# A new issue order of four engines in a fused attention-and-experts layer

## The reference, cut to what matters

```python
xn = layernorm(x)
q, k, v = split(xn @ W_qkv.T + b)            # 8 heads of 16
q, k, v = unit_length(q, k, v) * exp(i phase)
q, k = entangle(q), entangle(k)              # 3 depths, each head controlled by the one before it
for c in range(4):                           # 4 circuits
    s = |conj(q_i) . k_j|**2 * gain[c]       # 8 x 8 heads of one row
    w = sqrt(softmax(s) + 1e-12)
    out += sup[c] * clip(|sum_j w_ij v_j|) * its sign and phase
x + out @ W_out.T + b_out + experts(xn)
```

## Time and profile before

| what | value |
|---|---|
| median of 3 runs | 1520.07 us (1517.04 to 1521.86) |
| the profiled execution | 1518.64 us |
| its span, first to last instruction | 1516.9 us |
| granted TensorE clock, mean | 0.881 |
| busy, share of the span: VectorE, TensorE, ScalarE, GpSimd | 83%, 74%, 53%, 50% |
| opening, until block 0's first product | 111.1 us |
| steps between the first products of two blocks | 78 to 103 us |

### The profile page before, as it was taken

One profiled execution on the slowest core, in us unless ns is written; L12 is line 12 of the kernel. 1 busy time (PEld: TensorE's weight loads), 2 busy tenths in 40 slices (PEclk: granted clock), 3 DMA queues, 4 the chain that ended last, 5 costly groups with the idle time before them and its releaser, 6 DMA issues.

```text
span 1516.9 us, 19541 instructions
## 1 busy us (share of the span) xinstructions
PE 1118.7 (74%) x6049; PEld 867.6 (57%) x6049; DVE 1257.8 (83%) x1530; ACT 799.7 (53%) x1626; POOL 764.1 (50%) x596
## 2 busy tenths in 40 slices
PE   4476687968878797867969696784977878597734
PEld 2335475856657575655747475572755657475632
DVE  4634989898987998878988989696789998799975
ACT  3424466575646565464656656373545657365321
POOL 2073433365654455375455445647724545554683
PEclk9966798999989998888989899797989989899867
DMA  7333232342525252241423334152332516242111
GB/s 214 99 99 94 56 107 76 102 130 57 148 63 150 56 153 78 81 139 53 149 78 109 87 101 120 39 163 74 114 98 56 147 44 180 53 136 79 32 38 35
DMA packets 111559, 147.40 MB, mean 97 GB/s; under 512 B 15776, under 2 KB 85088, under 8 KB 110944
## 3 DMA queue, kind: packets, MB, share of 16 engines
q1 hardware_dynamic: 102240, 125.15, 27.6%
q0 software_dynamic: 8192, 16.79, 3.4%
q10 hardware_dynamic: 1024, 4.20, 2.1%
HBM read 113.95 MB, written 32.14 MB: 96 GB/s over the span
## 4 chain that ended last, share of the span: by engine, by line
PE 51%; POOL 13%; issue 12%; ACT 11%; DVE 10%; DMA 2%; SPq 1%; ACTq 0%; DVEq 0%; POOLq 0%
PE ps_t L739 8%; PE ps_r L788 8%; PE ps_h L660 7%; PE ps_f L668 6%; PE ps_q L739 6%; PE ps_t L746 4%; POOL prod L1276 3%; PE ps_k L726 3%; POOL rows_in L1302 3%; POOL got L1317 3%; POOL sqx L1267 2%; ACT hid L1124 2%; DVE pat L1697 1%; POOL prod L1284 1%; DVE xy L1489 1%
## 5 line engine op out<-in xcount | busy, mean ns | idle before, releaser
L1284 POOL TENSOR_TENSOR prod<-expo,vT 128x512 f32<-128x512 f32 x192 | 237.1, 1269 | 138.4 <-DVE u L1697 98.0
L788 PE MATMUL ps_r<-sqx,mats 128*128 128x512 f32 x256 | 163.8, 773 | 186.1 <-POOL sqx L1267 164.7
L1276 POOL TENSOR_TENSOR prod<-kq 128x1024 f32<-128x1024 f32 x64 | 150.0, 2366 | 291.7 <-ACT kq L1059 291.6
L1124 ACT ACTIVATE hid<-ps_h,w_tile 128x128 f32<-128x128 f32 x624 | 178.0, 370 | 145.7 <-PE ps_h L660 144.5
L660 PEld LDWEIGHTS ps_h<-turned,w_tile 128*128 128x128 f32 x1248 | 173.3, 208 | 79.1 <-issue 54.2
L1697 DVE TENSOR_REDUCE pat<-prod 128x128 f32<-128x2048 f32 x96 | 217.1, 2276 | 0.5
L660 PE MATMUL ps_h<-turned,w_tile 128*128 128x128 f32 x1248 | 182.4, 293 | 39.5 <-issue 19.9
L788 PEld LDWEIGHTS ps_r<-sqx,mats 128*128 128x128 f32 x256 | 54.2, 235 | 244.5 <-POOL sqx L1267 170.2
L1267 POOL TENSOR_TENSOR sqx<-sqx,sqy 128x512 f32<-128x512 f32 x64 | 87.3, 1384 | 204.6 <-ACT sqy L1039 143.7
L1673 DVE TENSOR_TENSOR prod<-expo,ps_v 128x2048 f32<-128x2048 f32 x80 | 180.7, 2280 | 7.8 <-PE ps_t L739 6.3
L1668 DVE TENSOR_TENSOR prod<-ps_q,kq 128x1024 f32<-128x1024 f32 x128 | 150.4, 1216 | 38.4 <-PE ps_q L844 21.4
(11 more groups left out here) (267 smaller groups left out, 2130.8 us busy)
## 6 DMA issues: line engine op xcount, KB each, us to landing
w_tile<-w_cat SPq DMA_DIRECT2D x156, 514.0 KB
x_tile<-rows_in SPq DMA_DIRECT2D x156, 64.0 KB, 2.8
rows_out<-turned SPq DMA_DIRECT2D x156, 64.0 KB
rows_in<-u SPq DMA_DIRECT2D x2, 2496.0 KB, 11.9
yacc<-in_L_attn_query_dram SPq DMA_DIRECT2D x16, 256.0 KB, 4.3
out_dram<-yacc SPq DMA_DIRECT2D x16, 256.0 KB, 3.1
x_sb<-in_L_attn_query_dram SPq DMA_DIRECT2D x11, 256.0 KB, 4.2
b_tile<-b_parts SPq DMA_DIRECT2D x156, 0.8 KB
```

Of the source, the lines that this page charges most:

```text
L788: nc.tensor.matmul(ps_r[:, bank, :], m, sqx[:, g, :], start=True, stop=True).then_inc(sig.sem, 1)
L1124: act.activation(hid[:, n % 2, c, :], ps_h[:, c, :], ACT.Gelu, bias=w_tile[:, n % WS, HID + HC * C + c:HID + HC * C + c + 1]).then_inc(hid ...
L1276: last = pool.tensor_tensor(set_of(2, part), q, other, ALU.mult)
L1284: last = pool.tensor_tensor(dst[:, at], w[:, at], v[:, at], ALU.mult)
```

## The change

Only the order of calls in the four loops differs; no call is added or dropped, and SyncE's list is the same. The lines with a minus are taken out where they stand, those with a plus put in; `if exists(...)` guards and lines that stay are mostly left out.

```diff
@@ TensorE
-k_operands(k, 1)
+q_operands(k, 1)
 sum_rows(routed)
+k_operands(k, 1)
+tiles(k, 0, 1)
+k_operands(k, 2)
 rank_rows(routed)
-q_operands(k, 1)
-tiles(k, 0, 1)
-k_operands(k, 2)
 tiles(k, 1, 2)
 q_operands(k, 2)
-tiles(k, 2, 3)
+k_operands(k, 3)
 mix_circuits(o)
-tiles(k, 3, 4)
+tiles(k, 2, 3)
 control_tiles(n)
+tiles(k, 3, 4)
+q_operands(k, 3)
 target_tiles(n)
-q_operands(k, 3)
 turn_m(o)
-k_operands(k, 3)
-tiles(k, 4, 5)
 project_out(o)
+tiles(k, 4, 5)
 grow_once(n)
 turn_x(j)
 grow_once_more(n)
 tiles(k, 5, 6)
+score(j)
 grow_twice(n)
 tiles(k, 6, 7)
 grow_twice_more(n)
 sums(k, ("weighted", 0))
 sums(k, ("weighted", 1))
 k_operands(n, 0)
-score(j)
 sums(k, ("weighted", 2))
 project(far, [0, 1])
-tiles(k, 7, 8)
-project(far, [2])
 q_operands(n, 0)
-sums(k, ("weighted", 3))
+tiles(k, 7, 8)
+project(far, [2])
 tiles(k, 8, 9)
 project(far, [3])
+sums(k, ("weighted", 3))
 tiles(k, 9, None)
@@ ScalarE
+copy_tile(k, 1)
 copy_sums(routed)
-copy_tile(k, 1)
-copy_v(k)
-tiles(k, 0, 1)
 abs_sign(o, 3)
+tiles(k, 0, 1)
+norm_sqrt(n)
+copy_v(k)
 router_softmax(routed)
-tiles(k, 1, 2)
+copy_tile(k, 2)
 ln_sd(j)
-norm_sqrt(n)
-copy_tile(k, 2)
+tiles(k, 1, 2)
+copy_tile(k, 3)
 tiles(k, 2, 3)
-tiles(k, 3, 4)
 control0(n)
-copy_tile(k, 3)
-tiles(k, 4, 5)
+tiles(k, 3, 4)
 copy_mT(o)
 control1(n)
+pass_first(n)
+tiles(k, 4, 5)
 layer_norm(j)
-pass_first(n)
 copy_out(o)
+turn(n)
+control2(n)
+score_exp(k)
+pass_last(n)
 copy_xT(j)
-turn(n)
-score_exp(k)
-control2(n)
-pass_last(n)
 tiles(k, 5, 6)
...
 tiles(k, 8, 9)
-abs_sign(k, 1)
 copy_proj(far, [3])
+abs_sign(k, 1)
 tiles(k, 9, None)
@@ GpSimd
+gather(first of the step)
 products(k, ("pattern", 2))
 scatter_part(k, 0)
-gather(first of the step)
 products(k, ("pattern", 5))
 sum_squares(n, sq1_ready, sum1_ready)
+gather(second and third of the step)
 scatter_part(k, 1)
 sum_squares(n, sq2_ready, sum2_ready)
-gather(second and third of the step)
+scatter_part(k, 2)
 products(k, ("weighted", 4))
 products(k, ("weighted", 5))
-scatter_part(k, 2)
+products(k, ("weighted", 6))
 scatter_part(k, 3)
-products(k, ("weighted", 6))
 gather(fourth of the step)
@@ VectorE
 products(k, ("pattern", 0))
+sums(k, ("pattern", 0))
 route(routed)
-layer_norm_stats(j)
 sums(o, ("weighted", 6))
-sums(k, ("pattern", 0))
+layer_norm_stats(j)
 norm_squares(n)
 products(k, ("pattern", 1))
+clip_and_mix(o)
 row_numbers(routed)
-clip_and_mix(o)
 normalise(n)
-sums(k, ("pattern", 2))
-products(k, ("pattern", 3))
 invert_sd(j)
+products(k, ("pattern", 3))
+route_gates(routed)
 measure(o)
+sums(k, ("pattern", 2))
 sums(k, ("pattern", 1))
-sums(k, ("pattern", 3))
 spread(n)
 products(k, ("pattern", 4))
+sums(k, ("pattern", 3))
 sums(k, ("pattern", 4))
...
 turned_states(n)
-route_gates(routed)
 probabilities(k)
...
 grown_twice(n, 1)
-products(k, ("weighted", 2))
 keep_scores(j)
+products(k, ("weighted", 2))
```

More of the change, by code:

```diff
@@ L875, in _ @@
                     k_operands(k, 2)
+                if routed is not None:
+                    rank_rows(routed)
                 tiles(k, 1, 2)
@@ L910, in _ @@
                 tiles(k, 5, 6)
+                if exists(j):
+                    score(j)
                 if exists(n):
@@ L1196, in _ @@
                     control1(n)
+                if exists(n) and exists(k):
+                    pass_first(n)
+                tiles(k, 4, 5)
                 if exists(j):
                     layer_norm(j)
-                if exists(n) and exists(k):
-                    pass_first(n)
                 if exists(o):
                     copy_out(o)
-                if exists(j):
-                    copy_xT(j)
                 if exists(n):
                     turn(n)
+                if exists(n):
+                    control2(n)
                 if exists(k):
@@ L1209, in _ @@
                 if exists(n):
-                    control2(n)
-                if exists(n):
                     pass_last(n)
+                if exists(j):
+                    copy_xT(j)
                 tiles(k, 5, 6)
@@ L1333, in _ @@
                 o, n = k - 1, k + 1
+                for b in gathered_at.get(k, [])[0:1]:
+                    gather(b)
                 if exists(k):
@@ L1336, in _ @@
                 scatter_part(k, 0)
-                for b in gathered_at.get(k, [])[0:1]:
-                    gather(b)
                 if exists(k):
@@ L1342, in _ @@
                     sum_squares(n, sq1_ready, sum1_ready)
+                for b in gathered_at.get(k, [])[1:3]:
+                    gather(b)
                 scatter_part(k, 1)
@@ L1345, in _ @@
                     sum_squares(n, sq2_ready, sum2_ready)
-                for b in gathered_at.get(k, [])[1:3]:
-                    gather(b)
+                scatter_part(k, 2)
                 if exists(k):
                     products(k, ("weighted", 4))
+                if exists(k):
                     products(k, ("weighted", 5))
-                scatter_part(k, 2)
-                scatter_part(k, 3)
                 if exists(k):
                     products(k, ("weighted", 6))
+                scatter_part(k, 3)
                 for b in gathered_at.get(k, [])[3:]:
@@ L1805, in _ @@
                     products(k, ("pattern", 0))
+                if exists(k):
+                    sums(k, ("pattern", 0))
                 if routed is not None:
                     route(routed)
+                if exists(o):
+                    sums(o, ("weighted", 6))
                 if exists(j):
                     layer_norm_stats(j)
-                if exists(o):
-                    sums(o, ("weighted", 6))
-                if exists(k):
-                    sums(k, ("pattern", 0))
                 if exists(n) and exists(k):
@@ L1817, in _ @@
                     products(k, ("pattern", 1))
+                if exists(o):
+                    clip_and_mix(o)
                 if routed is not None:
                     row_numbers(routed)
-                if exists(o):
-                    clip_and_mix(o)
                 if exists(n) and exists(k):
                     normalise(n)
+                if exists(j):
+                    invert_sd(j)
+                if exists(k):
+                    products(k, ("pattern", 3))
+                if routed is not None:
+                    route_gates(routed)
+                if exists(o):
+                    measure(o)
                 if exists(k):
@@ L1869, in _ @@
                     grown_twice(n, 1)
+                if exists(j):
+                    keep_scores(j)
                 if exists(k):
                     products(k, ("weighted", 2))
-                if exists(j):
-                    keep_scores(j)
                 if exists(k):
```

37 lines of the change are left out of this document (14 added, 23 removed).

## The result

The changed kernel takes 1481.8 us (1481.1 to 1485.3, 3 runs) against 1520.1 us: a ratio of 0.976 [0.972, 0.979], 38 us gained where 59 were forecast. The time lies inside the range of 1432 to 1504, but 21 us above the forecast, and it is nearer to rival A's 1497 than to the forecast itself.

The account below looks back on a forecast made before the run. It took VectorE's work, held unchanged, plus its 259.1 us of idle time as the bound. Gains less costs summed to 58.4 us, taking the kernel from 1520.07 to a forecast 1461 us, with a range of 1432 to 1504.

Parts of the forecast that it names:

- rival A: TensorE's list between weighted sums and key operands sets the step, so parts give half or less: 1497 us, chance 0.20.
- The paragraph on the port: VectorE's clip still meets GpSimd's product on a shared port, so its freed 0.64 us wait counts 0.
- part 6: Costs: exponentials behind second-control squarings -9 us, scores ahead of the second growing -2, step 3's border -3, step 15 0.
- Parts 1 to 3: GpSimd's list: first gather at the head 14.5 us, second between squares 21.9, weighted product 6 before the last scatter 7.
- part 5: Small ones: earlier spread before the first growing 6 us, norm_sqrt ahead of a tile 4, mixing and measure net 2.
- Part 4: Back half of a step: scores, query operands and weighted sum 3 reordered, ending waits mostly given back; 17 us gain.
- Mixing in step 11: Mixing ahead of a tile that waits for its rows would free 4 of 4.50 us.
- Step 3's border: Between tiles 7 and 8 the covering weighted sum is gone, so VectorE waits for a new group's rows: -3 us.
- Step 15's head gather: Gather waits for the last tile's store and the pattern product queues behind it: 0 us, bounds -4 to 3.
- B: Second growing, hung on turned_states, copy_xT and score, makes VectorE stand 6 us more per block: 1528 us, chance 0.09.
- C: Every named wait goes and nothing replaces it, 90 us or more: 1425 us, chance 0.06; copied keys stood against it.
- D: Stalls of the two gather moves return as other GpSimd stalls in the same steps, no change: 1520 us, chance 0.05.

Follow-up runs that it names:

- E1: Changed kernel with ScalarE's four exponentials put back ahead of the second control's squarings: 1469.8 us, ratio 0.967.
- E6: Changed kernel with the first combine of a step moved on VectorE behind turned_states, probabilities and value_phase: 1519.4 us, ratio 1.000.
- E7: E1 with GpSimd's first pattern product waiting for the next step's value vectors in steps without a scatter, and VectorE's pattern sums 1 and 2 swapped: 1450.7 us.
- E12: E8 with the router scores back in their old place on TensorE and VectorE: 1462.9 us, ratio 0.962.
- E2: Changed kernel with weighted sum 3 back ahead of tile 8 and the last projection on TensorE, abs_sign ahead of ScalarE's last projection copy: 1483.9 us.
- E8: E1 with the next step's tile 1 query and key operands ahead of the last expert tile on TensorE, copies on ScalarE likewise: 1452.5 us, ratio 0.957.
- E9: E1 with the router scores back in their old place on TensorE and VectorE: 1469.4 us, ratio 0.967.

## Why the prediction was right in its direction and short in its size

**The step that failed is in its first paragraph**: "the time is VectorE's work, which this change leaves as it is, plus its idle time". The idle part was nearly right: 53.5 us against a sum of 58.4. The work was not left as it was: it grew by 20.2 us. The paragraph on the port had the mechanism in hand and priced it at 0, since it asked about one instruction, the clip, and took GpSimd's product for one piece. It held the freed wait of 0.64 us for worth nothing; these 0.64 us are what puts the clip before GpSimd's second instruction, and it did not ask what is next then, though step 15 showed it. The clip gave back 15.4 us, the multiplication behind it took 20.2 us, and the combine, which nobody had looked at, took 21.5 us: the squarings put ahead of the exponentials (part 6) started GpSimd's add 3 us earlier, 579.96 - 578.73 = 1.2 us behind the combine's start instead of 583.33 - 579.08 = 4.3 in E1. E1, E6 and E7 show it. The rule of the Trainium skill (page "SBUF — State Buffer", section "Who interferes with whom"), that the second to come blocks fully, is in line with the rows of the clip, the multiplication and the combine, and not with the scaling of E12, which came first by 0.2 us and stood for 4.93. Applied to every instruction of VectorE that the change slid against GpSimd, and not to one, it would have pointed at this term. The runs show the blocking; that it happens at a port is what that page says, and no run here shows it.

**Parts 1 to 3** (14.5 + 21.9 + 7, and 6 of part 5, 49 us): the waits for weighted products and the first growing fell by 31.6 + 22.7 = 54 us. Right in place, and near in size. No wait over 1.4 us is left before the first growing, and none of 7 us before a weighted sum.

**Part 4** (17): scores and query operands fell by 25.1 + 15.9 us and keys rose by 26.9: 14 us. Right. That a step's second product hangs on all of TensorE's list is in line with E2; what the prediction took for fixed was where the expert tile stands in it, worth 17 us (E8).

**Part 5**: `norm_sqrt` in step 0 brought nothing (21.4 us against 20.2; 4 forecast): the wait did not follow its place. Mixing in step 11 freed its 4.5 us, but the waits for the first control rose from 5.1 to 9.6 us, with 5.49 of it in that step where there was 1.09.

**Part 6**: the exponentials came late in just the six steps named, 10.4 us against 9. The second growing rose from 11.1 to 18.1 us, 7 against 2; E9 puts the price of the early scores at 9. Step 3's border: 5.06 and 7.83 us where there were 4.49 and 3.95, 4.4 against 3. Step 15's head gather: taken at 0, with 4 us as its worst; it cost 7.3 us, since it sat 7.77 us on the last tile's store and then issued eight DMAs ahead of the product:

```profile
1388.87 0.99 POOL L1317 DMA_INDIRECT got<-rows_out,row_of  x1 [7.77 <-DMA rows_out<-turned]
...
1401.24 4.63 POOL L1276 TENSOR_TENSOR prod<-kq 128x1024 f32<-128x1024 f32 x2
```

**The rivals.** A (half given back) comes near in its number and not in its reason: the stalls went, and what came back is VectorE's own work. B is refuted: E9 prices its mechanism at about 9 us, not 66. C's gap was the keys, as named, and E8 shows that those waits could largely go, though two thirds of them come back as other waits. D is refuted.

Not settled: why E1's 16.7 us of faster combines and 10.4 us of ended waits yield 12 us, 15 in the profiled executions. Of the 12 us that are missing there, 6 are VectorE instructions that became longer (the exponentials' multiplication by 3.9, a small comparison in `value_phase` by 2.2) and the rest small waits for TensorE's growing and GpSimd's products.

## What to carry to other kernels

When an order of work changes, sum the busy time as well as the idle time: an instruction's duration depends on what the other engine runs beside it. Before moving work, list every VectorE instruction with two SBUF inputs (and those like the clip) that slides against a GpSimd instruction, and price each meeting with the time that GpSimd's instruction has left, or with two of them (E12). In the trace of before look for a step in which the new distance already occurs. A wait that keeps two such instructions apart can be worth more than the waiting that it costs (E7, 19 us).

## What the runs showed of the hardware

- What a meeting costs goes by GpSimd's instructions and not by VectorE's size: a scaling of 96 columns, 0.21 us alone, took 2.43 us in E8 (one of GpSimd's) and 4.93 us in E12 (both); eight small combines took 2.0 us more beside two of GpSimd's instructions and 4.0 more beside four.
- A VectorE product with one operand in PSUM was not slowed beside GpSimd (2.36 us at 542.57 in the changed kernel, and 2.36 at 542.58 in E7, where GpSimd stood idle), nor were two reductions (4.46 us at 567.07 in E1, beside GpSimd's add at 567.00).
- It goes both ways: GpSimd's pattern product took 5.68 us beside the clip and 4.67 us alone, its add 3.64 beside `turned_states` and 2.50 alone.
